# A transformer block's tail: FFN m-tiles placed between the last attention products, with two value products in a row

## The reference

```python
mod = (_silu(c) @ wmod).reshape(B, 6, 1, -1)          # sa, ca, ga, sb, cb, gb
h = _layernorm(x) * (1 + ca) + sa
x = x + ga * attention(h)       # 16 heads of 128, rotary, causal softmax, output projection
h = _layernorm(x) * (1 + cb) + sb
x = x + gb * ffn(h)
...
def _qlinear(x, wq, scale):
    W = (wq.astype(jnp.float32) - ZERO_POINT) * scale[:, None]
    return jnp.einsum('bsd,hd->bsh', x, W)
gate = _silu(_qlinear(x, wq_gate, s_gate))
return _qlinear(gate * _qlinear(x, wq_up, s_up), wq_down, s_down)
```

## Time and profile before

| | |
|---|---|
| median of 3 runs | 1066.7 us (1066.3 to 1068.06) |
| the profiled execution | 1067.72 us, span 1065.9 us |
| mean granted TensorE clock | 0.989 of 2.4 GHz |
| busy in the span | PE 96%, DVE 76%, ACT 63%, POOL 58% |
| unit 30, unit 31 | 26.64 us, 23.71 us |
| turn 6.0 of the ending to m-tile 8 | 57.9 us |

### The profile page before, as it was taken

The page is one execution under the profiler, slowest core; times in us unless marked ns, Lnnn a source line. Parts: engine busy times, 40 slices in busy tenths (PEclk is TensorE's granted clock), DMA queues, the critical chain, the costliest instruction groups (busy, mean ns, idle before and its releaser), DMA issues.

```text
span 1065.9 us, 20577 instructions
## 1 busy us (share of the span) xinstructions
PE 1028.2 (96%) x6368; PEld 918.8 (86%) x6368; DVE 810.5 (76%) x1707; ACT 670.7 (63%) x1443; POOL 622.6 (58%) x473
## 2 busy tenths in 40 slices
PE   6989999999999999999999999999999999988898
PEld 5779998899999998999899999999899999866676
DVE  6867777777777777777788777777777778779764
ACT  5466666666666666666666666666666666656642
POOL 2255755566566656665557556665667565655643
PEclk9899999999999999999999999999999999989999
DMA  9212111211112211221121112211122111410001
GB/s 284 77 30 65 46 41 40 68 43 43 35 36 64 50 39 40 69 50 39 31 64 45 40 40 70 49 40 30 39 60 50 39 41 40 142 40 1 11 30 42
DMA packets 41685, 55.99 MB, mean 53 GB/s; under 512 B 5204, under 2 KB 24724, under 8 KB 41620
## 3 DMA queue, kind: packets, MB, share of 16 engines
q1 hardware_dynamic: 41620, 55.30, 20.0%
HBM read 19.63 MB, written 2.10 MB: 20 GB/s over the span
## 4 chain that ended last, share of the span: by engine, by line
PE 87%; DVE 7%; issue 2%; ACT 1%; DMA 1%; POOL 0%; SPq 0%; DVEq 0%; ACTq 0%
PE ps_r L1182 17%; PE ps_r L1181 17%; PE ps_r L1180 17%; PE ps_t L1301 11%; PE ps_s L1182 6%; PE ps_s L1181 6%; PE ps_s L1180 6%; PE ps_s L1187 1%; PE ps_r L1187 1%; PE ps_s L1190 1%; PE ps_r L1189 1%; DVE xn L920 1%; DVE pT_lo L1029 1%; DMA swapped<-straight 1%; DVE ps_s L1056 1%
## 5 line engine op out<-in xcount | busy, mean ns | idle before, releaser
L563 POOL TENSOR_TENSOR swapped<-swapped,sin_sb 128x512 f32<-128x512 f32 x124 | 166.0, 1339 | 247.0 <-DMA swapped<-straight 247.0
L762 ACT ACTIVATE pT_hi<-ps_t 128x512 fp32r<-128x512 f32 (+3 forms) x384 | 186.5, 491 | 90.6 <-PE ps_t L1301 88.7
L1029 DVE TENSOR_TENSOR pT_lo<-ps_t,pT_hi 128x512 fp32r<-128x512 f32 (+3 forms) x384 | 202.1, 550 | 48.6 <-ACT pT_hi L762 48.5
L1056 DVE CUSTOM_DVE_ANT_0 ps_s<-ps_s,mask_wide 128x128 f32<-128x128 f32 (+7 forms) x256 | 194.5, 760 | 56.9 <-PE ps_s L1182 43.8
L570 POOL TENSOR_TENSOR qk_lo<-straight,qk_hi 128x512 fp32r<-128x512 f32 x124 | 161.8, 1318 | 110.4 <-ACT qk_hi L686 110.4
L773 ACT ACTIVATE probs<-ps_s,neg_max 128x128 f32<-128x128 f32 (+7 forms) x256 | 189.8, 742 | 33.1 <-DVE neg_max L1056 29.9
L1301 PE MATMUL ps_t<-ident,probs 128*128 128x128 f32 x1152 | 185.7, 275 | 9.1 <-DVE pT_lo L1029 9.1
L564 POOL TENSOR_TENSOR straight<-straight,cos_sb 128x512 f32<-128x512 f32 x124 | 180.4, 1454 | 0.0
L954 DVE TENSOR_TENSOR straight<-straight,swapped 128x512 f32<-128x512 f32 x126 | 128.8, 1022 | 33.1 <-POOL straight L564 32.8
L1301 PEld LDWEIGHTS ps_t<-ident,probs 128*128 128x128 f32 x1152 | 134.3, 140 | 13.5 <-issue 9.9
L1180 PE MATMUL ps_s<-qk_hi 128*128 128x512 f32 (+3 forms) x384 | 139.4, 363 | 0.5 <-ACT probs L773 0.4
(11 more groups left out here) (179 smaller groups left out, 2291.2 us busy)
## 6 DMA issues: line engine op xcount, KB each, us to landing
swapped<-straight SPq DMA_DIRECT2D x252, 128.0 KB, 2.3
x_in<-in_L_attn_x SPq DMA_DIRECT2D x4, 512.0 KB, 5.6
w_raw<-in_L_attn_Wk SPq DMA_DIRECT2D x8, 256.0 KB, 2.8
w_raw<-in_L_attn_Wq SPq DMA_DIRECT2D x8, 256.0 KB, 3.1
w_raw<-in_L_attn_Wv SPq DMA_DIRECT2D x8, 256.0 KB, 3.4
wo_all<-in_L_attn_Wo SPq DMA_DIRECT2D x1, 2048.0 KB, 12.3
wo_raw<-in_L_attn_Wo SPq DMA_DIRECT2D x8, 256.0 KB, 2.7
x<-in_L_attn_x SPq DMA_DIRECT2D x4, 512.0 KB, 4.0
```

Source lines behind the costliest of these rows:

```text
L563: pool.tensor_tensor(swapped[:, q, :], swapped[:, q, :], sin_sb[:, cs], ALU.mult)
L762: nc.scalar.activation(turned_at(ORDER[step], k0, k1)(pT_hi), ps_t[:, (T_FIRST[step] + j) % 2, 0:(k1 - k0) * P].rearrange("p (k q) -> p k ...
L1029: nc.vector.tensor_tensor(turned_at(t, k0, k1)(pT_lo), ps_t[:, (T_FIRST[step] + j) % 2, 0:(k1 - k0) * P].rearrange("p (k q) -> p k q", q=P ...
L1056: nc.vector.tensor_tensor_reduce(rows, rows, mask_wide[:, SEQ - n_keys:SEQ], -1.0, -MASKED, ALU.add, ALU.min, accum_out=neg_max[:, t:t + 1 ...
```

## The change

The ending is written as plans too. Units 29, 30 and 31 get plans of their own, and a 33rd, `ENDING`, in which the first five m-tiles of the FFN (and the sixth behind them) stand in TensorE's list between the last products: turns, ffn:0, P0, P1, ffn:1, the four W pieces, then ffn:2 to ffn:4, two turned x tiles, ffn:5. The branch on the weights' width moves ahead of this, so the first chunk has two matmuls per product as the others.

- The gate and up integers are loaded in unit 28 to 29 into hT's batch 0 space, and converted by ScalarE in unit 29 (down in 30). All weight transposes are pieces of `ps_r` in unit 30 (L0 to L5: pairs of gate and up tiles) and 31 (D0 to D2: pairs of down tiles); ScalarE copies each out in full, GpSimd copies the fp32r part (`late_high`, `down_high`). The subtractions of weights go.
- The transpose of the largest weight is the piece X of unit 31; VectorE reads it (`width`) behind the moments of chunk 0.
- Normalisation goes by chunk of 512 tokens: `x2_moments` (8 linked-in statistics and one add), `x2_roots` (a bit-shift guess and three Newton steps, twelve small VectorE operations, no square root), `normal` (four ScalarE activations). Chunk 0's stand in unit 31, chunk 1's and 2's moments in the ending, the rest beside m-tiles 6 to 13.
- The turned x tiles 0 to 3 are `ps_r` pieces H0 to H3; 4 to 7 follow m-tiles 9, 10, 14 and 15.
- Residuals of chunks 2 and 3 go from VectorE to GpSimd, before gu_lo of m-tile 0, and behind those of m-tiles 4 and 5.
- gate times up has four buffers instead of two.

```diff
+MOMENTS_AT = {9: 3}
+NEWTON_AT = {6: 2, 11: 3}
+NORMAL_AT = {8: 2, 13: 3}
+TURN_AT = {9: (4,), 10: (5,), 14: (6,), 15: (7,)}
+RESIDUAL_AT = {4: (3, 0), 5: (3, 1)}
...
+PLANS_30 = {
+    TENSOR_PLAN: """make:K0+ make:Q0+ scores:0 turn:6.0- turn:7.0- scores:1 scores:2 turn:7.1- make:P0- turn:0.0
+        make:P1- scores:3 turn:1.0 make:W00- make:K1+ scores:4 turn:1.1 make:W01- turn:2.0 make:Q1+
+        make:W10- scores:5 turn:3.0 make:W11- make:L0 turn:3.1 make:L1 turn:4.0 scores:6 make:L2 make:L3 turn:5.0 scores:7
+        make:L4 turn:5.1 make:L5""",
+    SCALAR_PLAN: """out:K0+ exp:7- turn:6.0- exp:0 out:Q0+ turn:7.0- turn:7.1- float:3 high:P0- turn:0.0 exp:1 exp:2
+        high:P1- high:K0+ high:Q0+ turn:1.0 out:K1+ turn:1.1 exp:3 turn:2.0 exp:4 out:Q1+ turn:3.0
+        exp:5 turn:3.1 out:L0 turn:4.0 out:L1 high:K1+ out:L2 turn:5.0 out:L3 exp:6 turn:5.1 out:L4 high:Q1+ out:L5""",
+    VECTOR_PLAN: """largest:0 max:0 turn:6.0- turn:7.0- turn:7.1- max:1 low:P0- add:K0+ max:2 turn:0.0 add:Q0+ largest:1
+        low:P1- max:3 sum:W00- turn:1.0 max:4 sum:W01- turn:1.1 turn:2.0 sum:W10- max:5 turn:3.0 sum:W11- add:K1+ turn:3.1
+        turn:4.0 max:6 largest:2 add:Q1+ max:7 turn:5.0 turn:5.1"""}
+PLANS_31 = {
+    TENSOR_PLAN: """make:K0+ make:Q0+ scores:0 turn:6.0- turn:7.0- scores:1 scores:2 turn:7.1- make:P0- turn:0.0
+        make:P1- scores:3 turn:1.0 make:W00- make:X scores:4 turn:1.1 make:W01- make:D0 turn:2.0
+        make:W10- scores:5 turn:3.0 make:W11- make:D1 turn:3.1 make:H0 turn:4.0 scores:6 make:H1 turn:5.0 scores:7
+        make:D2 turn:5.1""",
+    SCALAR_PLAN: """out:K0+ exp:7- turn:6.0- exp:0 out:Q0+ turn:7.0- turn:7.1- high:P0- turn:0.0 exp:1 exp:2
+        high:P1- turn:1.0 turn:1.1 exp:3 out:D0 turn:2.0 exp:4 turn:3.0 normal:0
+        exp:5 out:D1 turn:3.1 out:H0 turn:4.0 out:H1 exp:6 turn:5.0 out:D2 turn:5.1""",
+    VECTOR_PLAN: """max:0 turn:6.0- turn:7.0- turn:7.1- max:1 low:P0- max:2 turn:0.0 largest:3
+        low:P1- max:3 sum:W00- turn:1.0 moments:0 max:4 sum:W01- turn:1.1 width:X newton:0 turn:2.0 sum:W10- max:5 turn:3.0
+        sum:W11- turn:3.1 turn:4.0 max:6 max:7 turn:5.0 turn:5.1"""}
+ENDING = {
+    TENSOR_PLAN: """turn:6.0- turn:7.0- turn:7.1- ffn:0 make:P0- make:P1- ffn:1 make:W00- make:W01-
+        make:W10- make:W11- ffn:2 ffn:3 ffn:4 make:H2 make:H3 ffn:5""",
+    SCALAR_PLAN: """exp:7- turn:6.0- turn:7.0- turn:7.1- tanh:0 high:P0- normal:1 high:P1- tanh:1 gu:0 tanh:2 gu:1 tanh:3
+        gu:2 tanh:4 gu:3 out:H2 out:H3 tanh:5 gu:4""",
+    VECTOR_PLAN: """moments:1 turn:6.0- turn:7.0- turn:7.1- newton:1 ffn:0 low:P0- low:P1- ffn:1 sum:W00- sum:W01-
+        sum:W10- sum:W11- ffn:2 ffn:3 ffn:4 moments:2 ffn:5"""}
+UNIT_29 = {SCALAR_PLAN: """out:K0+ exp:7- turn:6.0- exp:0 out:Q0+ turn:7.0- turn:7.1- high:P0- turn:0.0 exp:1 float:0 exp:2
+        high:P1- high:K0+ high:Q0+ turn:1.0 float:1 out:K1+ turn:1.1 exp:3 turn:2.0 exp:4 out:Q1+ float:2 turn:3.0
+        exp:5 turn:3.1 turn:4.0 high:V0 high:K1+ high:V1 turn:5.0 exp:6 turn:5.1 high:Q1+"""}
...
+    last = {ALL_UNITS - 3: UNIT_29, ALL_UNITS - 2: PLANS_30, ALL_UNITS - 1: PLANS_31, ALL_UNITS: ENDING}
+    plan = last.get(u, {}).get(plan, plan)
...
+            sp.wait_ge(piece_made, PIECE_AT[("qk", ALL_UNITS - 3, 0, 1)] + 1)
+            for n, src in enumerate((wq_gate, wq_up)):
+                sp.dma_start(int_main[n][:, :, :], src[0:4 * P, :].rearrange("(m p) d -> p m d", p=P))\
+                    .then_inc(ints_ready[n], 16)
+                sp.dma_start(int_rest[:, n, 0, :], src[4 * P:5 * P, :]).then_inc(ints_ready[2], 16)
+                sp.dma_start(int_rest[0:HLAST, n, 1, :], src[5 * P:HID, :]).then_inc(ints_ready[2], 16)
+            run(Span(ALL_UNITS - 3, ALL_UNITS - 2))
+            for j in range(4):
+                sp.wait_ge(w_ready[j], PAIRS)
+            sp.dma_start(int_down[:, :, :], wq_down.rearrange("(k p) h -> p k h", p=P)).then_inc(ints_ready[3], 16)
+            run(Span(ALL_UNITS - 2, ALL_UNITS - 1))
...
+            def late_high(n):
+                which, first, size = late_span(n)
+                pool.wait_ge(late_full, n + 1)
+                pool.tensor_copy(wg_hi[which][:, :, first:first + size], wg_full[which][:, :, first:first + size])\
+                    .then_inc(late_ready, 1)
...
+            for n in range(len(LATE_PAIRS)):
+                late_high(n)
+            down_high(0)
+            h2_low(0)
+            down_high(1)
+            h2_low(1)
+            down_high(2)
+            def residual_of(n, half):
+                if half == 0:
+                    pool.wait_ge(y_added, 1 + 4 * (ALL_UNITS - 1) + 2 * (n - 1))
+                residual(n, half)
+            residual_of(2, 0)
+            residual_of(2, 1)
             for n in range(NCH * HM):
                 size = P if n % HM < HM - 1 else HLAST
-                for what, j in BESIDE.get(n, []):
-                    {"w": w_part_low, "h": h2_low}[what](j)
+                for j in ((2, 3) if n == 3 else TURN_AT.get(n - 1, ())):
+                    h2_low(j)
                 pool.wait_ge(gu_hi_ready, n + 1)
-                pool.tensor_tensor(gu_lo[0:size, n % GU, :], gu[0:size, n % 2, :],
-                                   gu_hi[0:size, n % GU, :].bitcast(F32), ALU.subtract).then_inc(gu_split, 1)
+                pool.tensor_tensor(gu_lo[0:size, n % GU, :], gu_at(n, size), gu_hi[0:size, n % GU, :].bitcast(F32),
+                                   ALU.subtract).then_inc(gu_split, 1)
+                if n in RESIDUAL_AT:
+                    residual_of(*RESIDUAL_AT[n])
...
+            def normal(n):
+                act.wait_ge(rstd2_ready, n + 1)
+                for t in range(4 * n, 4 * n + 4):
+                    ins = nc.scalar.activation(xn2[n][:, t % 4, :], x2[:, t, :], ACT.Identity, bias=shift_x2[:, t:t + 1],
+                                               scale=rstd[:, t:t + 1])
+                ins.then_inc(xn2_ready, 1)
...
+            for n in range(HM, NCH * HM):
+                gate_tanh(n)
+                gu_high(n - 1)
+                if n in NORMAL_AT:
+                    normal(NORMAL_AT[n])
+                for j in TURN_AT.get(n, ()):
+                    h2_out(j)
...
+            def x2_roots(n):
+                part = slice(4 * n, 4 * n + 4)
+                root_of = guess[:, part].bitcast(F32)
+                link(nc.vector.tensor_scalar(guess[:, part], var[:, part].bitcast(I32), 1, None, ALU.arith_shift_right))
+                link(nc.vector.tensor_scalar(guess[:, part], guess[:, part], -1.0, float(0x5f3759df), ALU.mult, ALU.add))
+                for step in range(3):
+                    link(nc.vector.scalar_tensor_tensor(newton[:, part], root_of, -0.5, root_of, ALU.mult, ALU.mult))
+                    link(nc.vector.tensor_tensor(newton[:, part], newton[:, part], var[:, part], ALU.mult))
+                    link(nc.vector.scalar_tensor_tensor(rstd[:, part] if step == 2 else root_of, newton[:, part], 1.5, root_of,
+                                                        ALU.add, ALU.mult))
+                nc.vector.scalar_tensor_tensor(shift_x2[:, part], mv[:, part, 0], -1.0, rstd[:, part], ALU.mult, ALU.mult)\
+                    .then_inc(rstd2_ready, 1)
...
+                elif old[0] == "late":
+                    pe.wait_ge(late_full, old[1] + 1)
+                elif old[0] == "down":
+                    pe.wait_ge(down_full, old[1] + 1)
+                elif old[0] == "h":
+                    pe.wait_ge(h2_hi_ready, old[1] + 1)
+                elif old[0] == "width":
+                    pe.wait_ge(wide_ready, 1)
...
+                ending = Span(ALL_UNITS, ALL_UNITS + 1)
+                for what, x, piece in ending.work(TENSOR_PLAN):
+                    if what == "ffn":
+                        gate_up(*piece, wide_weights)
+                    else:
+                        do(ending, what, x, piece)
                 for n in range(HM, NCH * HM):
                     chunk, m = divmod(n, HM)
-                    if m == 0:
-                        pe.wait_ge(h2_ready, chunk * KT + KT)
                     gate_up(n, wide_weights)
-                    beside(n)
+                    for j in TURN_AT.get(n, ()):
+                        turn_xn2(j)
                     if m in (1, 2):
-                        if chunk == 1 and m == 1:
-                            if wide_weights:
-                                pe.wait_ge(wf_late_ready, len(W_TILES) - W_EARLY)
-                            else:
-                                pe.wait_ge(wf_hi_ready, len(W_TILES))
+                        if n == HM + 1:
+                            pe.wait_ge(down_ready, DOWN_PAIRS)
                         down(chunk - 1, m - 1, wide_weights)
```

508 lines of the change are left out of this document (238 added, 270 removed).

## The result

| | before | changed |
|---|---|---|
| median | 1068.19 us (1066.3 to 1069.9, 8 runs) | 1070.48 us (1068.38 to 1073.12, 8 runs) |
| ratio to before, 95% interval | | 1.0028 [1.0015, 1.004] |
| profiled execution, its span | 1067.72, 1065.9 | 1068.38, 1066.6 |
| mean granted clock | 0.989 | 0.984 |

So the change costs 0.28%, a little more than what counted as no change. Repeated later, beside another kernel, it was 1.0024 [1.0015, 1.0034].

The account below looks back on a forecast made before the run. TensorE was taken as the bound up to the last two units, then waits, mostly on VectorE, and half-rate clock. Terms +1.8, +6.8, +1.5, -17.3 and +8.0 for later chunks gave +0.85: 1067.6 us against the median, range 1060 to 1075.

Parts of the forecast that it names:

- the clock rival: After four wait clusters (unit 31's middle and end, m-tiles 6-8, 12) TensorE stays longer at 1.2 GHz: 1073 us, chance 0.27.
- the sum: All stages of the kernel added: +0.85 us, 1067.6 against the median; its case 1064 to 1072, chance 0.46.
- Unit 30, +1.8: Six late pieces take 2.5 us of TensorE against 1.94 of waits; gate pieces need L4's and L5's banks: +1.8 us.
- Unit 31, +6.8 and 1.5: D0 waits 4.1 us for VectorE's width, ScalarE is last at the end: +6.8 us, plus 1.5 for port and clock.
- the port's 0.8: In unit 31, VectorE's moments or Newton steps may wait for GpSimd's copies: 0.8 us taken, 0 to 2.8 possible.
- The ending, -17.3: Turn 6.0 to the eighth m-tile takes 40.6 us for 57.9, GpSimd's gu_lo releasing down 0: -17.3 us.
- Later chunks, +8.0: GpSimd's order makes m-tile 12 wait 3.95 us, m-tile 18 1.75; half clock 1.6, moved turns 0.75: +8.0 us.
- The overlap rival: VectorE alone sets unit 31 (+3.8), and m-tile 12 waits at most 1 us with clock up: 1060 us, chance 0.27.

Follow-up runs that it names:

- e8: e7 with H0 and H1 moved from unit 31 behind the last turns, newton:0 and normal:0 later in unit 31: 1062.81 us, ratio to before 0.9963.
- e3: Changed kernel with moments:1 placed behind the low parts of turns 6.0, 7.0 and 7.1 on VectorE: 1068.95 us, ratio to before 1.0016.
- e1: Changed kernel with GpSimd's low parts of turned x tiles 4 to 7 one m-tile earlier: 1064.75 us, ratio to before 0.9969.
- e5: Changed kernel with the edits of e4 (including e1) and e3, plus width first and moments:0, newton:0 later in unit 31: 1059.96 us, ratio to before 0.9938.
- e9: e5 without the edits at m-tile 6 that e4 added, keeping the earlier lows of e1: 1060.40 us, ratio to before 0.9941.
- e2: Changed kernel with width ahead of moments:0 in VectorE's list of unit 31: 1067.86 us, ratio to before 1.0005.
- e4: e1 with H2 and H3 made and copied earlier, their GpSimd lows earlier, residual 3 one m-tile later: 1063.61 us, ratio to before 0.9974.
- e6: e5 with GpSimd's low parts of H2 and H3 one m-tile earlier still, ahead of gu_lo(1): 1060.84 us, ratio to before 0.9948.
- e7: e5 with residual 3 moved behind gu_lo(10) and (11) on GpSimd, chunk 3's norm and turns later: 1061.61 us, ratio to before 0.9949.

## Why the prediction was right

The forecast was 1067.6 with a range of 1060 to 1075. The measured 1070.48 lies in it, 2.9 above; the chance that stood highest, slower by over 0.2% (0.43, of which 0.27 was the clock rival's), is what came. It was +0.85 by the sum; +2.10 by the two profiles from the shared point. The four terms below are off by +0.8, +0.5, -1.5 and +1.4 us; that they come within 1.3 us together is in part luck. The mechanisms behind them are what the trace shows.

- **Unit 30, +1.8: +2.59.** The term that was under-sized is the six late pieces: 24 more instructions cost TensorE 28.43 - 24.70 = 3.73 us, where 2.5 were taken (the first four took 0.44 to 0.54 each, the last two, L4 and L5, 0.90 and 1.02); the waits fell from 1.94 to 0.8, as the step said.
- **Unit 31, +6.8 and 1.5: +8.81.** D0's wait of 4.1 was 4.04, its "width" at 942.4 in the old time was 943.66 in one that starts 1.2 later. Turn 6.0 was to be 8 to 12 us later than 947.73; it is at 957.73, 10.0 later, and 11.4 later when counted from unit 30's first scores. `normal` took 2.06 for 1.45; the late copies 0.61 for 1.2, so they were over before the moments began (938.1 and 939.2) and of the port's 0.8 only 0.44 was used: one Newton step beside D0's copy took 0.60 instead of 0.16. ScalarE was busy from 948.29 to turn 6.0 without a gap, as argued. But e8 shows that ScalarE's list isn't all: 2.7 us less on it gave 1.8.
- **The ending, -17.3: -18.79.** 39.1 us for 40.6. M-tile 6 waited 1.97 for 2.4; down 0 0.56 for 2.6, since TensorE came 1.4 later to it and GpSimd 0.8 earlier. That the wait is there and whose it is was right (e3 makes it 2.14).
- **Later chunks, +8.0: +9.49.** 3.54 for 3.95, 1.53 for 1.75, both released by hT_lo; e1 shows that the order is the cause. The half rate behind m-tile 12 was 6.4 us, and the sum had paid for 3.2: 1.4 us by the times above, which the other execution does not have. The stretch from m-tile 18 on, the same work in both, was 0.4 longer, 0.3 of it behind TensorE's last matmul.

**The clock rival** gave 1073 and was to decide from about 15 us of half rate. There were 16.5 us in the first profile and about 20 in the second, in the four places it named, so by its own sign it was met; but only one of the first profile's four stretches was long, two of the second's. The one price that a run shows is that behind m-tile 12, 2.4 and 1.0 us. Its time, 1073, was 2.5 too high, as the sum's was 2.9 too low. It was half right: the mean execution pays more than the sum said, about what separates 1067.6 from 1070.5, which the runs do not settle further. The Trainium skill, TensorE: Matmul & The Clock Gate, "HAM oscillation", by which short work between waits is thrown back to the low level again and again, agrees with what the four stretches show (granted 0.50 to 0.54, each from the end of a wait of 1.69 to 4.04 us on, with full rate between them). e5, with 12.9 us of waits, has 3.4 us of half rate in unit 31 and 3.4 behind m-tile 12.

**The overlap rival** was out in this kernel: neither of its conditions held. Its time was reached only with other orders, by e5 and e9 (1059.96 and 1060.40), and by the second of its conditions more than the first: e1, which takes GpSimd's wait at m-tile 12 down to 1.26, gives some 6 of the 9.4 us, while unit 31 is still 7.7 us longer in e5 than before.

"I am wrong if unit 31 grows by under 5 us, or if m-tile 12 starts without a GpSimd wait": it grew by 8.8, and the wait was 3.54. Of ScalarE's table loads there are three where there were seven, the four fewer that were forecast.

## What to carry to other kernels

When work is interleaved by hand into fixed queues, price each instruction by what the bounding engine waits for behind it: a norm's moments, a low part or a residual placed one position ahead of the one transfer that another engine needs can cost up to its whole length (here e2 and e3 got back about half), and moving it is free. But follow the next wait too: at m-tile 12 the wait taken away stayed away, while at m-tile 6, where GpSimd's run has no gap, it came back at other places, through VectorE (e4). And compare two profiles from a point with the same work done: up to unit 30 these profiles differ by up to 3.7 us, more than the change does.

## What the hardware showed that was not expected

Timelines of VectorE and GpSimd of the changed kernel: the two steps of the first guess on 128x4 elements, beside three GpSimd instructions in a row.

```profile
991.12 0.81 DVE L1154 TENSOR_SCALAR guess<-var 128x4 int32<-128x4 int32 x1
991.96 4.80 DVE L1155 TENSOR_SCALAR guess<-guess 128x4 int32<-128x4 int32 x1
```

```profile
991.86 1.28 POOL L716 TENSOR_TENSOR gu_lo<-gu_a,gu_hi 64x512 fp32r<-64x512 f32 x1
993.11 2.38 POOL L664 TENSOR_TENSOR x<-x,y 128x1024 f32<-128x1024 f32 x1
995.45 1.28 POOL L716 TENSOR_TENSOR gu_lo<-gu_b,gu_hi 128x512 fp32r<-128x512 f32 x1
```

A tiny step took 4.80 us instead of the 0.17 that it took at 943.78, and ended at 996.76, with GpSimd's last instruction (996.73). The earlier trace rows had shown one such step wait for one GpSimd instruction (1.20); it was not foreseen that it can wait through three that follow each other. The Trainium skill, SBUF — State Buffer, "Who interferes with whom", names tensor_scalar among the operations that may take the shared ports and says that the loser waits for the whole instruction of the other; the trace agrees on the operation, and shows more than one instruction waited for. TensorE did not pay for it here: it has no wait over 0.2 us between 993.25 and 1009.02. In e4 to e6 it did, where such a step took 6.86 to 6.88 us beside four GpSimd instructions, and in e7, without residual 3 in that run, it took 0.92.

Copies of 512 columns from float32 to fp32r took GpSimd 0.61 us, half of what a subtract of the same size took (1.27).
